# Decay counted from a chunk's end, negated gates, and two DVE affine steps moved to ScalarE

## The reference, cut to what matters

```python
xx = shift(xn) - xn
xm = xn + xx * (low_rank(xn + xx * maa_x) + maa)          # four mixes: rg, wa, k, v
r, k, v, g = xrg @ Wr.T, xk @ Wk.T, xv @ Wv.T, tanh(xrg @ G1.T) @ G2
w  = -softplus(-(time_decay + w2)) - 0.5                   # log-decay before exp
kk = normalise_per_head(k + tanh(xk @ K1.T) @ K2)
a, ma, mk = sigmoid(...), sigmoid(...), sigmoid(...)
k  = k * ma + k * a * (1 - ma)
k  = k * exp(w * mk);  b = -kk * a;  decay = exp(-exp(w))
# per head, token by token:
s = s * decay + (s @ kk) b^T + v k^T;   y = s @ r
y = groupnorm_per_head(y) * ln_w + ln_b + (sum(r*k*faaaa)) * v
x = x + (y * g) @ Wo.T
# then a layer norm, rows quantised to int8 steps, and a product with weight_q, added to x with a bias
```

## Time and profile before

| | us |
|---|---|
| median of 3 runs (lowest, highest) | 3842.75 (3841.96, 3844.0) |
| the profiled execution's own time | 3840.55 |
| its span | 3838.8 |
| PE busy, share of the span | 3423.7, 89% |
| DVE busy | 3368.9, 88% |
| POOL busy | 1765.3, 46% |
| ACT busy | 1277.2, 33% |
| mean granted TensorE clock | 0.984 |

### The profile page before, as it was taken

How to read it: one execution, slowest core, us unless ns; L and a number is a source line. 1 busy time by engine, 2 the same in 40 slices (tenths; PEclk the granted TensorE clock), 3 DMA queues, 4 the chain that set the end, 5 groups by cost and what they waited for, 6 DMA issues and landing times.

```text
span 3838.8 us, 226260 instructions
## 1 busy us (share of the span) xinstructions
PE 3423.7 (89%) x104641; PEld 2955.7 (77%) x104704; DVE 3368.9 (88%) x7619; ACT 1277.2 (33%) x2885; POOL 1765.3 (46%) x1861
## 2 busy tenths in 40 slices
PE   6999999899988998998999988999998999989885
PEld 6777777787777787777777777877777778777774
DVE  5898888898988888989999888998898998988985
ACT  3333233233332333333333323333333333233331
POOL 4444444444444444444454444444444444444442
PEclk9999999999999999999999999999999999999997
DMA  3000000000000000000000000000000000000000
GB/s 103 12 15 20 15 17 20 12 20 20 12 20 16 16 20 12 20 20 12 20 19 14 20 15 18 20 12 20 20 12 20 18 15 20 15 18 20 12 15 16
DMA packets 39559, 73.25 MB, mean 19 GB/s; under 512 B 9812, under 2 KB 10836, under 8 KB 38616
## 3 DMA queue, kind: packets, MB, share of 16 engines
q1 hardware_dynamic: 38616, 58.77, 5.6%
HBM read 41.97 MB, written 16.78 MB: 15 GB/s over the span
## 4 chain that ended last, share of the span: by engine, by line
PE 44%; DVE 43%; issue 8%; ACT 4%; SPq 1%; DMA 0%; POOL 0%; POOLq 0%; DVEq 0%; ACTq 0%
PE bank L1115 10%; PE bank L1122 10%; PE bank L1245 5%; PE bank L1359 5%; DVE pm L740 3%; DVE mix L765 3%; DVE w_ffn_int L887 3%; PE bank L1323 3%; DVE pw L740 3%; DVE kt L740 2%; PE bank L1309 2%; ACT L532 2%; PE bank L1349 2%; DVE cum L788 2%; DVE lnsig L787 2%
## 5 line engine op out<-in xcount | busy, mean ns | idle before, releaser
L532 ACT ACTIVATE u_sb<-bank 128x128 f32<-128x128 f32 x256 | 71.1, 278 | 905.9 <-PE bank L1339 902.7
L1280 PE MATMUL bank<-pw,w_ffn_int 32*32 32x48 f32 x16384 | 247.8, 204 | 128.3 <-DVE pw L740 117.4
L1280 PEld LDWEIGHTS bank<-pw,w_ffn_int 32*32 32x32 f32 x16384 | 207.1, 105 | 170.3 <-DVE w_ffn_int L887 74.4
L1122 PE MATMUL bank<-lo,w_maa 128*128 128x128 f32 x2048 | 321.2, 290 | 6.1 <-DVE xm_v L775 3.5
L1122 PEld LDWEIGHTS bank<-lo,w_maa 128*128 128x128 f32 x2048 | 266.3, 193 | 60.2 <-issue 32.1
L397 POOL TENSOR_TENSOR qkT<-w_ffn_int,rk 128x512 f32<-128x512 f32 x64 | 90.9, 1420 | 478.6 <-DVE rk L931 478.6
L1115 PE MATMUL bank<-xm_v,w_v 128*128 128x128 f32 x2048 | 278.2, 285 | 5.3 <-issue 5.1
L1359 PE MATMUL bank<-w_o,yc 128*128 128x512 f32 x512 | 269.6, 630 | 9.6 <-DVE yc L740 9.0
L1115 PE MATMUL bank<-xm_rg,w_r 128*128 128x128 f32 x2048 | 268.7, 279 | 0.7 <-issue 0.7
L1323 PE MATMUL bank<-km,vT 32*32 32x96 f32 x8192 | 257.5, 246 | 11.9 <-issue 11.4
L413 POOL TENSOR_TENSOR kmod<-gma,kmod 128x512 f32<-128x512 f32 x64 | 81.6, 1275 | 393.5 <-DVE kmod L802 393.5
(11 more groups left out here) (185 smaller groups left out, 9144.1 us busy)
## 6 DMA issues: line engine op xcount, KB each, us to landing
xin<-in_x SPq DMA_DIRECT2D x128, 128.0 KB, 2.7
xres<-in_x SPq DMA_DIRECT2D x128, 128.0 KB, 2.7
out<-o_sb SPq DMA_DIRECT2D x128, 128.0 KB
w_ffn_int<-in_weight_q SPq DMA_DIRECT2D x1, 2048.0 KB, 9.6
w_k<-in_Wk SPq DMA_DIRECT2D x1, 1024.0 KB
w_r<-in_Wr SPq DMA_DIRECT2D x1, 1024.0 KB
w_v<-in_Wv SPq DMA_DIRECT2D x1, 1024.0 KB
w_o<-in_Wo SPq DMA_DIRECT2D x1, 1024.0 KB, 12.9
```

Of the source, the lines that this page charges most:

```text
L532: return nc.scalar.activation(out_, in_, func, **kw)
L1122: ins = mm(bank[:, o * TOK:(o + 1) * TOK], weights[:, o * P:(o + 1) * P], hidden[:], start=True, stop=True)
L1280: ins = mm(rb[h][q, 3 * HALF * n:3 * HALF * (n + 1)], pt[q, g, :], pw[q, g].rearrange("p j t -> p (j t)"), start=True, stop=True)
```

## The change

The decay sum is scanned backwards within a chunk, so `pinv` (now 33 wide, shifted by one) is the decay from a token to the chunk's end, `pdec` its inverse. Keys and removal directions times `pinv` are then already what enters the state, and `kl`, `bl` and their products go; in return the state that PE reads must be `s_old` (state times the chunk's whole decay). The a and ma gates are taken as sigmoid(-x) and the key negated, so that b = (g-1) kk pinv and k = (g g' - 1)(-k) pinv z are each one DVE instruction with both operands in SBUF. The floor of sig becomes ACT's bias. Two affine steps go to ACT: `xn` (DVE only makes -mean*rstd) and the four head affines. On POOL `decayed_state(m, 1, h)` moves ahead of `norm2_rstd` and the mix of XV.

```diff
@@ POOL
-            def key_gate(i):
-                pool.wait_ge(v_k1, count(i, 1, 1))
-                nc.gpsimd.tensor_tensor(kmod[:], gma[:], kmod[:], ALU.subtract).then_inc(g_k2, 1)
-                pool.wait_ge(g_k2, count(i, 1, 1))
-                pool.wait_ge(a_k, count(i, 1, 1))
-                mul(kmod[:], kmod[:], kraw[:]).then_inc(g_k3, 1)
-
-            def removal_and_decay(i):
+            def kept_keys(i):
+                pool.wait_ge(v_k, count(i, 1, 0))
+                pool.wait_ge(a_ma, count(i, 1, 1))
+                mul(kept[:], ga[:], gma[:]).then_inc(g_keep, 1)
+
+            def undecayed(i):
+                pool.wait_ge(a_pinv, count(i, 1, 1))
+                mul(kmod[:], by_chunk(kraw), pinv[:, :, 1:]).then_inc(g_kp, 1)
                 pool.wait_ge(v_kkn, count(i, 1, 1))
-                mul(ga[:], ga[:], kk[:]).then_inc(g_b0, 1)
-                pool.wait_ge(g_k3, count(i, 1, 1))
+                mul(kkp[:], by_chunk(kk), pinv[:, :, 1:]).then_inc(g_kkp, 1)
+                pool.wait_ge(g_kp, count(i, 1, 1))
                 pool.wait_ge(a_ew, count(i, 1, 1))
-                mul(kmod[:], kmod[:], z[:]).then_inc(g_k4, 1)
+                mul(kmod[:], kmod[:], by_chunk(z)).then_inc(g_kz, 1)
...
-            def enter(m):
-                pool.wait_ge(v_pl, count(m, 1, 1))
-                pl = plast[:].unsqueeze(2).to_broadcast([P, G, CHUNK])
-                pool.wait_ge(v_k, count(m, 1, 1))
-                mul(kl, kt[:], pl).then_inc(g_kl, 1)
-                mul(bl, bt[:], pl).then_inc(g_bl, 1)
...
@@ POOL tile_step
                 if solve:
-                    enter(m)
                     for h in range(2):
                         decayed_state(m, 0, h)
                     bonus(m)
                 if project:
-                    key_gate(i)
+                    kept_keys(i)
...
                 if project:
-                    removal_and_decay(i)
+                    undecayed(i)
                 if mix:
                     mixed_inputs(j, XWA, XK)
-                if finish:
-                    norm2_rstd(n)
-                if mix:
-                    mixed_inputs(j, XV, XV)
                 if solve:
                     for h in range(2):
                         decayed_state(m, 1, h)
+                if finish:
+                    norm2_rstd(n)
+                if mix:
+                    mixed_inputs(j, XV, XV)
@@ ACT
+            def normalised(i):          # after mk_gate(i), before power1(m, 0)
+                act.wait_ge(v_shift1, count(i, 1, 1))
+                act.wait_ge(p_xT, count(i, 1, 0))
+                run(xn[:], xin[:], ACT.Identity, scale=rs1[:, 1:2], bias=shift1[:]).then_inc(a_xn, 1)
...
-                act.wait_ge(v_sigc, count(i, 1, 1))
-                run(lnsig[:], lnsig[:], ACT.Ln).then_inc(a_lnsig, 1)
+                act.wait_ge(a_sig, count(i, 1, 1))
+                act.wait_ge(v_w, count(i, 1, 0))
+                run(lnsig[:], sig[:], ACT.Ln, bias=sig_floor[:]).then_inc(a_lnsig, 1)
...
+            def head_affine(n):         # between queries(i) and values(i)
+                act.wait_ge(v_z1, count(n, 1, 1))
+                for k in range(KB):
+                    c = slice(k * TOK, (k + 1) * TOK)
+                    ins = run(yc[:, c], yc[:, c], ACT.Identity, scale=ln_w[:, k:k + 1], bias=ln_b[:, k:k + 1])
+                ins.then_inc(a_affine, 1)
@@ DVE
-                V.tensor_scalar(xn[:], xin[:], mv1[:, 0:1], rs1[:, 1:2], ALU.subtract, ALU.mult)
+                V.scalar_tensor_tensor(shift1[:], mv1[:, 0:1], -1.0, rs1[:, 1:2], ALU.mult, ALU.mult)
...
-                V.tensor_scalar(lnsig[:], sig[:], SIG_FLOOR, None, ALU.max).then_inc(v_sigc, 1)
-                V.tensor_tensor_scan(cum[:], chunk_reset[:], sig[:], 0.0, ALU.mult, ALU.add)
+                V.tensor_tensor_scan(cum[:, ::-1], chunk_reset[:], sig[:, ::-1], 0.0, ALU.mult, ALU.add)
...
-                V.scalar_tensor_tensor(kmod[:], gma[:], -1.0, ga[:], ALU.add, ALU.mult)
...
-                V.scalar_tensor_tensor(bt[:], by_chunk(ga), -1.0, by_chunk(pinv), ALU.mult, ALU.mult)
-                tt(kt[:], by_chunk(kmod), by_chunk(pinv), ALU.mult)
+                V.scalar_tensor_tensor(bt[:], by_chunk(ga), -1.0, kkp[:], ALU.add, ALU.mult)
+                V.scalar_tensor_tensor(kt[:], by_chunk(kept), -1.0, kmod[:], ALU.add, ALU.mult)
...
-                dve.wait_ge(g_kl, count(m, 1, 1))
-                V.transpose(km[:, :, 2, :], kl).then_inc(v_klT, 1)
-                dve.wait_ge(g_bl, count(m, 1, 1))
-                V.transpose(pm[:, :, 2, :], bl).then_inc(v_blT, 1)
+                dve.wait_ge(v_k, count(m, 1, 1))
+                V.transpose(km[:, :, 2, :], kt[:]).then_inc(v_klT, 1)
+                V.transpose(pm[:, :, 2, :], bt[:]).then_inc(v_blT, 1)
...
-                    ins = V.tensor_scalar(yc[:, c], yc[:, c], ln_w[:, k:k + 1], ln_b[:, k:k + 1], ALU.mult, ALU.add)
@@ PE
-                pe.wait_ge(v_state, count(m, STEPS, step(c, h)))
+                pe.wait_ge(g_sold, count(m, STEPS, step(c, h)))     # and reads s_old in place of the state
```

More of the change, by code:

```diff
@@ L175, in rwkv_ffn_kernel @@
             sem(f"p_{n}") for n in "xT lo xm hid hg z a ma mk k kkk v r".split())
-        (v_st1, v_xn, v_xx, v_mix, v_xm, v_sigc, v_w, v_cum, v_kk, v_sqT, v_kss, v_ss, v_rn, v_kkn, v_a, v_b, v_k1,
+        (v_st1, v_shift1, v_xx, v_mix, v_xm, v_w, v_cum, v_kk, v_sqT, v_kss, v_ss, v_rn, v_kkn, v_a, v_b,
          v_wm, v_k, v_q) = (
             sem(f"v_{n}") for n in
-            "st1 xn xx mix xm sigc w cum kk sqT kss ss rn kkn a b k1 wm k q".split())
-        (a_carry, a_xT, a_lo, a_hid, a_hg, a_z, a_sig, a_a, a_ma, a_mk, a_k, a_sq, a_lnsig, a_p, a_pinv,
+            "st1 shift1 xx mix xm w cum kk sqT kss ss rn kkn a b wm k q".split())
+        (a_xn, a_carry, a_xT, a_lo, a_hid, a_hg, a_z, a_sig, a_a, a_ma, a_mk, a_k, a_sq, a_lnsig, a_p, a_pinv,
          a_lnss, a_rn, a_ew, a_v, a_r) = (
             sem(f"a_{n}") for n in
-            "carry xT lo hid hg z sig a ma mk k sq lnsig p pinv lnss rn ew v r".split())
-        g_rs1, g_xm, g_k2, g_k3, g_k4, g_b0 = (sem(f"g_{n}") for n in "rs1 xm k2 k3 k4 b0".split())
+            "xn carry xT lo hid hg z sig a ma mk k sq lnsig p pinv lnss rn ew v r".split())
+        g_rs1, g_xm, g_keep, g_kp, g_kz, g_kkp = (sem(f"g_{n}") for n in "rs1 xm keep kp kz kkp".split())
         (p_sb, p_sk, p_p1, p_p2, p_p3, p_t3, p_t, p_rhs, p_u, p_s, p_g) = (
@@ L455, in decayed_state @@
             def decayed_state(m, c, h):
+                if c == 0 and h == 0:
+                    pool.wait_ge(v_pl, count(m, 1, 1))
                 pool.wait_ge(v_state, count(m, STEPS, step(c, h)))
@@ L496, in tile_step @@
                 if project:
-                    removal_and_decay(i)
+                    undecayed(i)
                 if mix:
                     mixed_inputs(j, XWA, XK)
+                if solve:
+                    for h in range(2):
+                        decayed_state(m, 1, h)
                 if finish:
@@ L559, in keys @@
                 act.wait_ge(p_k, count(i, 1, 1))
-                act.wait_ge(g_k4, count(i, 1, 0))
-                run(kraw[:], fb[0][:], ACT.Copy).then_inc(a_k, 1)
+                act.wait_ge(g_kp, count(i, 1, 0))
+                run(kraw[:], fb[0][:], ACT.Copy, scale=-1.0).then_inc(a_k, 1)
             def decay_gate(i):
@@ L817, in undecayed @@
             def undecayed(i):
-                dve.wait_ge(g_b0, count(i, 1, 1))
-                dve.wait_ge(a_pinv, count(i, 1, 1))
-                V.scalar_tensor_tensor(bt[:], by_chunk(ga), -1.0, by_chunk(pinv), ALU.mult,
-                                       ALU.mult).then_inc(v_b, 1)
-                dve.wait_ge(g_k4, count(i, 1, 1))
-                tt(kt[:], by_chunk(kmod), by_chunk(pinv), ALU.mult).then_inc(v_k, 1)
+                dve.wait_ge(g_kkp, count(i, 1, 1))
+                V.scalar_tensor_tensor(bt[:], by_chunk(ga), -1.0, kkp[:], ALU.add, ALU.mult).then_inc(v_b, 1)
+                dve.wait_ge(g_keep, count(i, 1, 1))
+                dve.wait_ge(g_kz, count(i, 1, 1))
+                V.scalar_tensor_tensor(kt[:], by_chunk(kept), -1.0, kmod[:], ALU.add, ALU.mult).then_inc(v_k, 1)
             def decayed(i):
```

79 lines of the change are left out of this document (37 added, 42 removed).

## The result

Side by side on one chip, the changed kernel took 3857.07 us (median of 17 runs, 3847.0 to 3875.98) and the kernel before 3839.34 us (17 runs, 3835.11 to 3846.33): a ratio of 1.005, 95% interval 1.0036 to 1.0063. It is slower by half a per cent. The time lies inside the range of 3775 to 3890, but on the other side of no change than the forecast of 3826; what happened is rival 1 (3872), on a somewhat smaller scale. The changed kernel's profiled execution is its fastest run, 3847.0 us with a span of 3845.3.

The account below looks back on a forecast made before the run. PE and DVE, both 90% busy, bound the kernel by leading in turn, with DVE and POOL contending for a port. Per tile -2.25 + 1.08 + 0.9 = -0.27 us, times 61 is -16.5, from 3842.75 to 3826; range 3775 to 3890.

Parts of the forecast that it names:

- rival 1: Powers' piece: DVE's first spread loses the port to POOL's weighted bonus; +0.48 us a tile, 3872 us; chance 0.30.
- the term of -2.25 us a tile in the powers' piece: From `km(1)` through the powers: DVE's savings cut PE's waits, 2.58 us a tile at most, by 2.25.
- the first spread's race for the port: Powers' piece: spread at about 2.53 us, POOL's weighted bonus at 2.50 after `km(1)`; if lost, the spread waits 1.13.
- `x2n` was to end at 3.68 after its zero: Quantiser's piece, zero 0.35 us ahead of `state(0,0)`: `x2n` ends at 3.68 behind POOL's power and `xm_v`; 1.08 a tile.
- PE's wait for `rhs_sb`: Before solve_step(1): PE's wait was to grow to 2.3 to 2.8 us as `x2n` comes later.
- `xx` and `mix`: DVE, powers' piece: with POOL's bonus earlier and key gate gone, 0.96 and 2.03 us fall to 0.68 and 1.12.
- The reversed scan: DVE's decay sum in the powers' piece: listed as unknown; 1.21 us forwards, at the dearest twice that allowed.
- The clock: PE behind the gap before solve_step(1): granted clock falls in most tiles, 0 to 1.45 us a tile, 0.9 taken.
- the foretold band: PE's mean granted clock of 0.96 to 0.97 if it falls in most tiles.
- the falls in the powers' piece: PE's clock falls during the powers: taken as few and let go, since PE gets denser there.
- the Identity with scale and bias from pointers: On ACT: `xn` takes 0.63 to 0.73 us and just fits; the four affines take 0.9 to 1.4, costing nothing.
- rival 3: Savings don't reach PE, whose gaps in the powers become issue gaps and ACT waits; +1.0 us a tile, 3904; chance 0.10.

Follow-up runs that it names:

- run 2: Changed kernel with DVE's bonus transpose moved behind the first spread, so POOL's weighted bonus starts after it: 3830.69 us, ratio 0.9971 to the kernel before.
- run 1: Changed kernel with POOL's second-norm power (norm2_rstd) put back ahead of its decayed_state products: 3685.41 us, ratio 0.9595 to the kernel before.
- Run 6: Changed kernel with twelve unread 128x128 products added on PE between from_state and solve_step(1): 3812.01 us, ratio 0.9909 to the kernel before.
- run 7: Kernel before with decayed_state ahead of norm2_rstd and the mix of XV on POOL, plus twelve unread PE products before solve_step(1): 3930.33 us, ratio 1.0219.
- run 3: Changed kernel with both norm2_rstd ahead of decayed_state on POOL and DVE's bonus transpose behind the first spread: 3643.11 us, ratio 0.9472 to the kernel before.
- run 9: Changed kernel with norm2_rstd ahead of decayed_state, bonus transpose behind the first spread, and POOL's kk*pinv ahead of kraw*pinv: 3643.18 us, ratio 0.9478.
- run 8: Kernel before with only the sig floor as ACT's bias and the four head affines on ACT: 3791.95 us, ratio 0.9859.
- run 4: Kernel before with only POOL's order changed, decayed_state(m,1,h) ahead of norm2_rstd and the mix of XV: 3966.37 us, ratio 1.0329.

## Why the prediction was wrong

**The step that failed** is the term of -2.25 us a tile in the powers' piece. It took the first spread's race for the port as won, on an estimate of 2.53 for the spread against 2.50 for POOL's bonus, both after `km(1)` starts. The traces have 2.53 and 2.51, and POOL was first in every tile but the last. The term is -1.39, close to the -1.5 of rival 1. With the race out of the way (run 2) PE's waits for `pw` are 0.64 a tile, where the forecast had them near zero; the term is then -1.94, and the time 3831. The other 0.3 us a tile were too much even with the race won. The lost race is worth 26 us in the changed kernel and 42 in run 1's, and the first of these is most of the 31 between forecast and result. The prediction had written both times down and put its forecast on the one that its own numbers were against. Two estimates 0.03 us apart say little; what they did say was "lost".

**Right, by its steps.** `x2n` was to end at 3.68 after its zero and ended at 3.67, with the 1.0 us idle for the power. The two `state` sums take 0.29 and 0.37. PE's wait for `rhs_sb` was to be 2.3 to 2.8 and is 2.53; it rose by 1.47 where `x2n` is 1.08 later. Some of the difference is that from_state no longer waits for DVE's `state`, which was 8.7 us in 49 tiles, 0.18 a tile, so that PE gets to the wait sooner; the rest of the difference isn't shown. `xx` and `mix` fell from 2.99 us to 1.81 (1.2 foretold). The reversed scan costs 1.22 us. There is no further table load: 197 in both kernels. The Trainium skill's page ScalarE: Activation LUTs, section Table sets: the hidden batching unit, has identity in every set; the traces agree, with these 197 loads.

**The clock** was to cost 0.9 us a tile. Run 6 gives 0.74 and run 7 0.6, both as lower bounds, since the products hold up the solve by 0.30 and 0.34 us a tile; with these added it is 0.9 to 1.0 (an estimate). The falls come where they were foretold, behind the gap, and the mean clock of 0.967 is in the foretold band. What the prediction took for few, the falls in the powers' piece, were a third of those before (7 of 24); they are gone.

**Too low:** the Identity with scale and bias from pointers. `xn` takes 0.80 us where I took 0.63 to 0.73, and the four affines 1.64 where I had 0.9 to 1.4. `xn` ends at 2017.27 and just fits: the copy of `pw` starts 2.22 us after `km(1)` in the kernel before, where it waits for PE, and as late here (the median over the tiles of either trace). So it isn't the longer `xn` that lost the race for the spread. The affines have room: POOL waits 5.0 us for them in all 64 tiles together. The Trainium skill's page ScalarE: Activation LUTs, section What ACT_TABLE_LOAD costs, has the price: 186 ns and 0.833 ns a column with immediates, and about 93 ns for each pointer operand. For 512 columns with two pointers I estimate 799 ns by that page, and for 128 columns 479. The traces agree: 803 and 483 ns. The prediction overlooked it.

**How it adds up.** The waits and the clock in the traces sum to -1.39 + 1.47 - 0.18 + 0.74 = +0.64 us a tile, and the times say 17.7 / 61 = +0.29. By the two profiled executions, from which the waits are, it is even less, 6.5 / 61 = +0.11. The sum lacks an item, and the clock's price isn't what the clock adds to PE's busy time. PE's busy time in the changed kernel's page shows it:

```profile
PE 3448.0 (90%) x104641; PEld 2992.2 (78%) x104704; DVE 3207.0 (83%) x7235; ACT 1422.2 (37%) x3205; POOL 1581.5 (41%) x1735
```

Against 3423.7 us before, PE is busy for 24.3 us more, +0.40 a tile, and idle for 397.3 us in place of 415.1, -0.29 a tile. The two make the +0.11. Of the idle time the waits named above are -0.10, and a wait for `yc` (4.4 us in 49 tiles) is +0.09; the item left out is PE's idle time put down to "issue", which fell from 73.8 to 57.6 us in the 49 tiles, -0.33. It did not fall everywhere: at the powers' product L1298 (now L1302) it rose from 6.3 to 17.5 us, so there a part of the saved wait for `pw` did turn into an issue gap, as rival 3 had it. Why the issue gaps fell elsewhere isn't shown.

## What to carry to other kernels

Before an instruction is moved on GpSimd, write down what VectorE starts within a microsecond of it: in the races here the later one waited until the other's instruction had ended, and hundredths decided which. Cost such a race at its full price and its place: before an instruction that TensorE waits for it was worth 0.4 to 0.7 us a tile here (runs 2 and 3), elsewhere nothing (run 9). A change whose parts look good by their busy time and that measures as nothing deserves an attempt at the order of its queues before it is dropped: here two swaps turned +0.5% into -5.3%.

## What the runs showed of the hardware

- A VectorE product of two SBUF tensors (the spread), or a tensor_scalar on one (`x2n`), and a GpSimd product: the first to start has the port for all of its time, also when it leads by 0.02 us (2017.59 against 2017.61). The Trainium skill's page SBUF — State Buffer, section SBUF: two separate sides, says so: an exclusive lock, held for its whole instruction by whichever starts first. The traces agree, with the 1.53 us of the spread. The one that waits ends sooner behind the other than its own duration would have it: the spread (0.42 alone) 0.28 us after POOL's product, `x2n` (0.53 alone) 0.28 after `xm_v`.
- The scan, with one input in bf16, is held up in the same way (1.94 us for 1.21, run 8).
- A scan over reversed columns costs what a forward one does: 1215 ns in the mean of 64, against 1.21 us.
- With a TensorE gap of 2.5 to 2.7 us in each tile, where it was about 1.1, the mean clock was 0.967 for 0.984 (and 0.960 in run 4, which differs from the kernel before in GpSimd's order alone). Filling the gap with idle products took it to 0.992, above that of the kernel before. Work that does nothing made the kernel 1.2% quicker. Where a gap can't be closed this is worth a try, though closing it was worth four times as much (172 us against 45).
